# Delta rule: the mixer's taps on ScalarE and VectorE, and the projections as three fp32r products

## The chip, the cores and the metric

The kernel runs on one core of a Trainium2 chip. The metric is the device time of one execution in microseconds; lower is better. Engines are called by the profile's short names: PE (TensorE), PEld (its weight loads), ACT (ScalarE), DVE (VectorE), POOL (GpSimd), SP (SyncE, which here only issues transfers).

## What is computed

The reference is one transformer block on x of shape (8, 512, 256): attention with a bias from a small MLP, then a gated delta rule, then two mixtures of experts. The change lies in the delta rule; of it, this matters here (h is the attention's output, one batch of 512 rows by 256):

```python
def short_conv(x, w):                # 4 taps per channel
    ...
    return y * jax.nn.sigmoid(y)
def fractal_mixer(x, conv_w):
    out = 2.0 * x
    for i in range(4):
        dil = 2 ** i
        x_shift = jnp.pad(x, ((0, 0), (dil, 0), (0, 0)))[:, :l, :]
        out = out + x_shift * conv_w[i, :, 0] + x * conv_w[i, :, 1]
    return out
q = short_conv(x @ Wq, conv_q)       # k and v in the same way
...                                  # rotary, l2norm, chunks of 32 rows:
S_new = g * S + k.T @ (u - w @ S)    # one state per head, 16 chunks in a row
...
frac = rmsnorm(fractal_mixer(x, frac_conv_w), mixer_norm_w)
```

## The kernel before, in words

Three phases follow one another: attention (0 to 1094 us of the profiled span), the delta rule (1099 to 1750) and the mixtures (1755 to the end). `attention_phase` writes its output turned, as `hT`, to DRAM; `delta_phase` reads one batch of it at a time into `h` (two buffers), with the 256 channels as two blocks (`KD`) of 128 partitions and the 512 rows along the free dimension.

`delta_phase` is a pipeline over the eight batches. Each engine works through a hand-written list of named pieces (`PE_ROUND`, `ACT_ROUND`, `DVE_ROUND`, `POOL_ROUND`, L1825 to L1876), once per round, in exactly that order. An entry (name, i, lag) works in round r on batch r - lag: lag NX = -1 is the next batch (first four projections, gates), IN = 0 the batch that comes in, F = 1 the one after it (inverse, u and w), R = 2 the recurrence, K = 3 the output. Twelve rounds run, from -1 to 10; rounds 3 to 6 hold pieces of every lag. The engines meet only through semaphores, so a piece that waits holds up all that stands behind it on its engine. PE's results go through a ring of five PSUM banks (`RING`) in PE's order: a bank is filled again once its reader is through.

The pieces that matter:

- "step" i on PE (L2126) and "S" i on DVE (L2406) are the recurrence over 16 chunks. Step i waits for S i-1, S i for step i. All other pieces stand between them.
- "proj" (L1978): a projection is 2 matmuls in fp32 (one for each block of channels), which the profile shows as 4 MATMULs of 512 columns. ACT copies it to `proj` and makes the first tap of the convolution (L2189, L2193); "conv" on DVE adds three more (L2292); "silu" on ACT.
- "mixer" (L2001): for each of 4 row tiles and 2 channel blocks, 5 matmuls of h, shifted by 1, 2, 4, 8 and 0 rows, against diagonal matrices `diag` of the taps, so that the sum comes out turned, rows on partitions. The profile shows 20 MATMULs for a tile. ACT's "frac" reads it (sum of squares, copy to `xg`), then "fve" on DVE, "frs" on POOL, and "xg" on DVE. All are IN pieces.
- After the projections: "z" (turn q and k), "rota"/"rotb" on DVE (L2304, L2316) and "rot" on POOL (rotary; rotb needs POOL's part, L2319), "rsq" (ACT), "rss" (DVE), "rrn" (POOL), "qk" (DVE), "qkT" (PE turns, ACT copies), "gram" (PE), "low" (DVE, L2355). SP then sends `low` through DRAM into `A0`, POOL inverts it ("inv", L2496, the last piece of POOL's list), and SP brings the result back as `TT1` for "T1", "Z" and "TZ" of the next round. POOL's next round begins with "kb", "gxm", "ors", "nb" and then "rot".
- "core" (PE) and "x1" (DVE) are the output of batch r - 3; `vk` (values and scaled keys) has two buffers.

Of the kernel before, what the change touches and what calls it, by code (L numbers as in the profile page):

```python
# [97 lines left out]
def delta_inputs(nc, ctx, a, sem):  # L98
# [5 lines left out]
    t = {"wqkv": sb("wqkv", [P, KD, 3 * D]), "wsm": sb("wsm", [P, KD, NG]), "smb": sb("smb", [P, NG]),  # L104
# [16 lines left out]
    t["in"], t["h0_in"], t["loads"] = sem("delta_in"), sem("delta_h0_in"), loads  # L121
    return t
# [15 lines left out]
def attention_phase(nc, a, ident, delta, mixture, bias_rows, hT_dram, inv_dram):  # L138
# [6 lines left out]
    with ExitStack() as ctx:  # L145
# [197 lines left out]
        with nc.Block() as block:  # L343
# [227 lines left out]
            def _(dve):  # L571
# [28 lines left out]
                for name, t in steps:  # L600
# [158 lines left out]
                    elif name == "hn":  # L759
                        dve.wait_ge(s["out_rstd"], t + 1)  # L760
                        if t > 0:
                            dve.wait_ge(full[1], filling["hT", t - 1, 1])
                        dve.tensor_scalar(hn[:], FB[0][:, 0:D], mv2[:, 0:1], rstd2[:], ALU.subtract,
                                          ALU.mult).then_inc(s["hn_ready"], 1)

            @block.scalar
            def _(act):
# [26 lines left out]
                for name, t in steps:  # L794
# [96 lines left out]
                    elif name == "hT":  # L891
# [6 lines left out]
                        last.then_inc(s["hT_ready"], 1)  # L898

# [772 lines left out]
def delta_phase(nc, a, ident, delta, mixture, hT_dram, xg_dram, low_dram, inv_dram, x1_dram):  # L1672
# [5 lines left out]
    with ExitStack() as ctx:  # L1678
        sb, bank, sem, sems = space(nc, ctx, "d")
        wqkv, wsm, smb, conv, frac, cos, sin, rot, mixw, strict, causal, chunk_of, side, eye16, corner, wo, onw, x = (  # L1680
            delta[n] for n in ("wqkv", "wsm", "smb", "conv", "frac", "cos", "sin", "rot", "mixw", "strict", "causal",
                               "chunk_of", "side", "eye16", "corner", "wo", "onw", "x"))
        own = sb("own", [P, KD])
        diag = sb("diag", [P, KD, 5, P])
# [3 lines left out]
        half = sb("half", [P, TT * H2])  # L1688
        h = [delta["h0"], sb("h1", [P, KD, PAD + L])]
        xg = sb("xg", [P, TT, D])  # L1690
# [5 lines left out]
        fsq = sb("fsq", [P, TT, D])  # L1696
# [27 lines left out]
        vk = sb("vk", [P, 2, TT, H2, 2, DH])  # L1724
# [27 lines left out]
        x_in = sem("x_in")  # L1752
        proj_psum = sem("proj_psum")
# [7 lines left out]
        nb_ready = sem("nb_ready")  # L1761
        mixer_psum = sem("mixer_psum")
# [60 lines left out]
        NS = NCH - 1  # L1823

        PE_ROUND = [  # L1825
            ("step", 0, R), ("fast", 0, R), ("M", 1, R), ("qp", 0, R), ("proj", 4, IN), ("au", 0, R),
            ("step", 1, R), ("fast", 1, R), ("M", 2, R), ("mixer", 0, IN), ("M", 3, R),
# [3 lines left out]
            ("step", 5, R), ("fast", 5, R), ("hold", 0, K), ("hold", 1, K), ("hold", 2, K), ("hold", 3, K), ("onT", 0, K), ("onT", 1, K), ("z", 3, IN), ("mixer", 1, IN),  # L1831
            ("step", 6, R), ("fast", 6, R), ("TZ", 0, F), ("core", 0, K), ("au", 3, R),
            ("step", 7, R), ("fast", 7, R), ("qkT", 0, IN), ("uw", 0, F), ("attn", 0, F),
            ("step", 8, R), ("fast", 8, R), ("mixer", 2, IN), ("qkT", 1, IN), ("uw", 1, F),
            ("step", 9, R), ("fast", 9, R), ("core", 1, K), ("qkT", 2, IN), ("uw", 2, F),
            ("step", 10, R), ("fast", 10, R), ("mixer", 3, IN), ("uw", 3, F), ("qkT", 3, IN),
# [7 lines left out]
            ("M", 2, R), ("osq", 0, K), ("silu", 2, IN), ("M", 3, R), ("frac", 0, IN),  # L1844
# [3 lines left out]
            ("onT", 0, K), ("onT", 1, K), ("z", 3, IN), ("rsq", 1, IN), ("frac", 1, IN),  # L1848
# [20 lines left out]
            ("S", 12, R), ("attn", 2, F), ("low", 1, IN), ("attn", 3, F), ("xg", 0, IN),  # L1869
            ("S", 13, R), ("vb", 0, IN), ("conv", 0, NX), ("xg", 1, IN),  # L1870
            ("S", 14, R), ("vb", 1, IN), ("conv", 1, NX), ("xg", 2, IN), ("gates", 0, NX), ("xg", 3, IN)]
        POOL_ROUND = [
            ("kb", 0, F), ("gxm", 0, F), ("ors", 0, K), ("nb", 0, IN), ("rot", 0, IN), ("rot", 1, IN), ("rrn", 0, IN),
            ("rot", 2, IN), ("rrn", 1, IN), ("rot", 3, IN), ("rrn", 2, IN), ("rrn", 3, IN), ("frs", 0, IN),
# [5 lines left out]
        def drained(name, i, b):  # L1880

            return {"fast": None, "hold": None, "proj": (proj_ready, 6 * b + i + 1), "gates": (gates_read, b + 1),
                    "mixer": (frac_copied, TT * b + i + 1), "z": (zm_ready, TT * b + i + 1),
# [21 lines left out]
        with nc.Block() as block:  # L1905
            @block.sync
            def _(sp):
                for r_ in range(B + 3):
                    bi, bf, bk = r_, r_ - 1, r_ - 3
                    if bi < B - 1:  # L1910
                        if bi > 0:
                            sp.wait_ge(mixer_psum, TT * bi)
                        sp.dma_start(h[(bi + 1) % 2][:, :, PAD:], hT_dram[bi + 2]).then_inc(h_in[(bi + 1) % 2], 16)
# [36 lines left out]
                    if bi < B:  # L1950
# [316 lines left out]
            def _(dve):  # L2267
# [19 lines left out]
                for name, i, b in pieces(DVE_ROUND):  # L2287
# [308 lines left out]
```

## Time and profile before

| what | us |
|---|---|
| median of 3 runs (lowest to highest) | 2610.37 (2606.3 to 2613.95) |
| the profiled execution: its time | 2605.69 |
| its span, first to last instruction | 2603.9 |
| PE busy | 2413.8 (93%) |
| DVE busy | 1696.0 (65%) |
| POOL busy | 1334.0 (51%) |
| ACT busy | 1216.3 (47%) |

Shares are of the whole span. A busy PE is one with matmuls under way; their ends are modelled. A row of a timeline reads: start, duration, engine, line, operation, output<-inputs, shape, count, and in brackets the idle time of the engine before it and what ended that. In a row that merges several instructions the duration is from the first one's start to the last one's end. A table by windows gives for each stretch the busy time of every engine with its count of instructions, then the granted clock of PE (1.00 is 2.4 GHz, 0.50 is 1.2 GHz).

### The profile page before, as it was taken

The page shows a single profiled execution, that of the slowest core. Times are in us where ns is not written, and L with a number is a line of the kernel's source. Part 1 is how long each engine was busy: PE and PEld are TensorE (multiplying, and loading weights), DVE is VectorE, ACT ScalarE, POOL GpSimd, SP SyncE. Part 2 cuts the span into 40 slices and gives each one's busy share as a digit, 9 for nine tenths or more (in the row PEclk, how much of TensorE's full clock was granted, in tenths as well). Part 3 has the DMA queues.
Part 4 walks back from the last instruction along what each step waited for, and adds up shares of the span by engine and source line. Part 5 has one row for each costly group of instructions (what it writes and reads, how often), then busy time and mean ns, then how long its engine had stood idle before and what let it go on. Part 6 is the DMA issues. An engine that isn't in the chain of part 4 may idle for free. (4 is left out here: it accounts for less than half of the span.)

```text
span 2603.9 us, 56605 instructions
## 1 busy us (share of the span) xinstructions
PE 2413.8 (93%) x20854; PEld 2007.2 (77%) x20854; DVE 1696.0 (65%) x4060; ACT 1216.3 (47%) x3095; POOL 1334.0 (51%) x1465
## 2 busy tenths in 40 slices
PE   4899999999999999878999999988899999999998
PEld 3788888888888888756777877756677778778776
DVE  4576777767677767576767767326756746747664
ACT  2656666666666666455444445114333333332332
POOL 3676776767676767256555555214522323322322
PEclk8999999999999999989999999988999999999999
DMA  4000100000000000012112111206112112212211
GB/s 141 7 10 9 45 17 11 9 10 10 10 10 9 9 5 5 15 31 45 42 47 49 36 53 43 55 31 187 33 52 68 62 42 74 66 42 62 64 39 58
DMA packets 156688, 105.05 MB, mean 40 GB/s; under 512 B 85168, under 2 KB 134832, under 8 KB 156416
## 3 DMA queue, kind: packets, MB, share of 16 engines
q1 hardware_dynamic: 131072, 62.83, 8.9%
q10 hardware_dynamic: 25344, 38.60, 4.8%
q8 instruction: 170, 2.79, 0.4%
q14 instruction: 102, 0.84, 0.1%
HBM read 80.51 MB, written 20.88 MB: 39 GB/s over the span
## 5 line engine op out<-in xcount | busy, mean ns | idle before, releaser
L920 POOL TENSOR_TENSOR a_bm<-a_bias,a_mask_add 128x512 f32<-128x512 f32 (+3 forms) x512 | 437.8, 871 | 191.0 <-DVE a_nm L674 186.0
L1529 POOL TENSOR_TENSOR m_hid_part<-m_hid,m_hid_part 128x512 fp32r<-128x512 f32 x176 | 239.5, 1361 | 564.1 <-ACT m_hid_part L1438 561.0
L830 ACT ACTIVATE a_S<-a_S,a_nm 128x512 f32<-128x512 f32 (+3 forms) x512 | 289.2, 565 | 346.4 <-DVE a_nm L674 343.6
L674 DVE CUSTOM_DVE_ANT_0 a_S<-a_S,a_bm,a_nsn 128x512 f32<-128x512 f32 (+3 forms) x512 | 275.4, 545 | 141.2 <-PE a_S L438 136.9
L461 PE MATMUL a_O<-a_v,a_PT 128*128 128x64 f32 x2560 | 342.4, 265 | 0.0
L461 PEld LDWEIGHTS a_O<-a_v,a_PT 128*128 128x128 f32 x2560 | 328.4, 193 | 0.0
L1450 ACT ACTIVATE m_hid<-m_G 128x512 f32<-128x512 f32 x176 | 105.4, 599 | 408.4 <-PE m_G L1384 371.3
L438 PE MATMUL a_S<-a_kT,a_qT 128*128 128x384 f32 (+3 forms) x1024 | 284.3, 359 | 3.5 <-DVE a_nm L674 3.0
L1401 PE MATMUL m_Y<-m_hid_part,m_down_high 128*128 128x512 f32 x704 | 257.3, 406 | 11.9 <-POOL m_hid_part L1529 11.1
L1611 DVE TENSOR_TENSOR m_hid<-m_hid,m_U 128x512 f32<-128x512 f32 x176 | 121.0, 687 | 223.6 <-PE m_U L1384 189.7
L1384 PE MATMUL m_G<-m_in,m_gate_high 128*128 128x512 f32 x704 | 251.5, 398 | 1.6 <-POOL m_up_low L1523 1.6
L1384 PE MATMUL m_U<-m_in,m_up_high 128*128 128x512 f32 x704 | 250.8, 397 | 1.7 <-DVE m_hid L1611 1.7
L448 PE MATMUL a_T<-s_ident,a_S 128*128 128x128 f32 x1280 | 227.0, 275 | 12.2 <-ACT a_PT L839 11.3
L448 PEld LDWEIGHTS a_T<-s_ident,a_S 128*128 128x128 f32 x1280 | 160.3, 140 | 42.2 <-ACT a_S L830 15.7
L438 PEld LDWEIGHTS a_S<-a_kT,a_qT 128*128 128x128 f32 x1024 | 164.1, 192 | 18.7 <-DVE a_nm L674 6.5
L1401 PEld LDWEIGHTS m_Y<-m_hid_part,m_down_high 128*128 128x128 f32 x704 | 133.4, 189 | 47.7 <-issue 15.8
L1384 PEld LDWEIGHTS m_U<-m_in,m_up_high 128*128 128x128 f32 x704 | 132.8, 189 | 34.9 <-DVE m_hid L1611 2.8
L1384 PEld LDWEIGHTS m_G<-m_in,m_gate_high 128*128 128x128 f32 x704 | 133.0, 189 | 34.5 <-POOL m_up_low L1523 2.1
L839 ACT COPY a_PT<-a_T 128x128 f32<-128x128 f32 (+3 forms) x384 | 156.2, 407 | 0.0
L1384 PE MATMUL m_G<-m_in,m_gate_low 128*128 128x512 f32 x352 | 140.2, 398 | 0.0
L1401 PE MATMUL m_Y<-m_hid_part,m_down_low 128*128 128x512 f32 x352 | 139.8, 397 | 0.0
L525 PE MATMUL a_F<-a_wqkv,a_xnT 128*128 128x512 f32 (+1 forms) x576 | 133.8, 369 | 5.9 <-POOL a_wqkv L944 3.7
(314 smaller groups left out, 5240.2 us busy)
## 6 DMA issues: line engine op xcount, KB each, us to landing
m_spread<-s_w ACTq DMA_DIRECT2D x64, 256.0 KB, 3.3
m_spread<-s_w ACTq DMA_DIRECT2D x128, 128.0 KB, 2.9
a_x<-in_x SPq DMA_DIRECT2D x32, 128.0 KB, 2.1
s_hT<-a_hT SPq DMA_DIRECT2D x32, 128.0 KB, 2.1
d_x<-in_x SPq DMA_DIRECT2D x8, 512.0 KB, 4.8
d_h<-s_hT SPq DMA_DIRECT2D x8, 512.0 KB, 5.4
s_xg<-d_xg SPq DMA_DIRECT2D x8, 512.0 KB, 3.1
d_x<-s_xg SPq DMA_DIRECT2D x8, 512.0 KB, 4.5
```

The lines of the kernel that those rows point to most:

```text
L438: last = pe.matmul(o_s[:, 0:w], qT[:, tile % 2, h], kT[tile // TT % 2][i][:, 0:w], start=i == 0, stop=i == 1)
L448: last = pe.transpose(TB[n % 2][:, j * P:(j + 1) * P], S[:, n % S_SLOTS, j * P:(j + 1) * P], ident[:])
L461: last = pe.matmul(OB[h // 8][:, (h % 8) * DH:(h % 8 + 1) * DH], PT[:, n % PT_SLOTS, j * P:(j + 1) * P], v[tile // TT % 2][:, j], start=j ...
L525: last = pe.matmul(f[:, 0:cols.stop - cols.start], xnT[i][:, k], wqkv[j][:, k, cols], start=n == 0, stop=n == len(terms) - 1)
L674: dve.tensor_tensor_reduce(S[:, n % S_SLOTS, 0:w], SB[n % 2][:, 0:w], bm[:, n % BM_SLOTS, 0:w], -1.0, nsn[:, tile % 2, h:h + 1], ALU.add, ...
L830: act.activation(S[:, n % S_SLOTS, 0:w], S[:, n % S_SLOTS, 0:w], ACT.Exp, scale=-1.0, bias=nm[:, tile % 2, h:h + 1], accum_out=den[:, tile ...
L839: act.copy(PT[:, n % PT_SLOTS, 0:w], TB[n % 2][:, 0:w]).then_inc(s["probsT_act"], 1)
L920: pool.tensor_tensor(bm[:, n % BM_SLOTS, 0:w], bias[:, h, L - w:L], mask_add[b % 2][:, 0:w], ALU.add).then_inc(s["bm_ready"], 1)
L1384: last = pe.matmul(dst[q % 2][:, :], wts[m][j][:, k, item], x[i][:, k], start=(i, j, k) == TERMS[0], stop=(i, j, k) == TERMS[-1])
L1401: last = pe.matmul(YB[k][:, :], down[m][j][:, item, k * P:(k + 1) * P], hid_part[i][:, q % H_SLOTS], start=item == 0 and i + j == 0, stop= ...
L1529: pool.tensor_tensor(hid_part[1][:, q % H_SLOTS], hid[:, q % G_SLOTS], hid_part[0][:, q % H_SLOTS].bitcast(F32), ALU.subtract).then_inc(hi ...
L1611: dve.tensor_tensor(h, h, UB[q % 2][:, :], ALU.mult).then_inc(mult_up, 1)
```

## The change

The mixer's sum is made by ACT (the unshifted tap, scaled, into a new buffer `mx`) and DVE (four shifted taps added in place); PE only turns `mx`. PE's turning, "frac", "fve", "frs" and "xg" move to lag F, one round later. The projections take both operands as fp32r, split into a high part (the cast) and a low part (the rest): high by high, weights' low by high, high by the input's low, so 6 matmuls of 512 columns. The input is split once a batch by two pieces "hs": ACT casts the high part, DVE subtracts it. The weights are split once, during attention. `vk` keeps one buffer, which "vb" and "kb" fill once "uw" of the batch before has been read.

```diff
@@ attention_phase, DVE and ACT
+                        if t == 4 * TT:      # behind "hn"
+                            dve.wait_ge(delta["high_ready"], 1)
+                            dve.tensor_tensor(delta["w_low"][:], delta["wqkv"][:], delta["w_high"][:].bitcast(F32),
+                                              ALU.subtract).then_inc(delta["low_ready"], 1)
...
+                        if t == 3 * TT:      # behind "hT"
+                            act.wait_ge(delta["in"], 16 * len(delta["loads"]))
+                            act.copy(delta["w_high"][:], delta["wqkv"][:]).then_inc(delta["high_ready"], 1)
@@ PE_ROUND: mixer 0 to 3 keep their places, IN becomes F
-            ("step", 10, R), ("fast", 10, R), ("mixer", 3, IN), ("uw", 3, F), ("qkT", 3, IN),
+            ("step", 10, R), ("fast", 10, R), ("mixer", 3, F), ("uw", 3, F), ("qkT", 3, IN),
@@ ACT_ROUND: frac 0 to 3 become F, and
-            ("frac", 2, IN), ("qkT", 1, IN), ("uw", 1, F),
-            ("qkT", 2, IN), ("uw", 2, F), ("silu", 5, IN),
-            ("frac", 3, IN), ("uw", 3, F), ("qkT", 3, IN),
+            ("frac", 2, F), ("qkT", 1, IN), ("uw", 1, F), ("tap", 0, IN),
+            ("hs", 0, NX), ("qkT", 2, IN), ("uw", 2, F), ("silu", 5, IN),
+            ("tap", 1, IN), ("frac", 3, F), ("uw", 3, F), ("qkT", 3, IN),
@@ DVE_ROUND: fve and xg become F, and
-            ("S", 9, R), ("qk", 3, IN), ("conv", 5, IN),
-            ("S", 10, R), ("x1", 1, K),
-            ("S", 11, R), ("fve", 0, IN), ("attn", 1, F), ("low", 0, IN),
+            ("S", 9, R), ("qk", 3, IN), ("hs", 0, NX), ("conv", 5, IN),
+            ("S", 10, R), ("x1", 1, K), ("mix", 0, IN),
+            ("S", 11, R), ("fve", 0, F), ("attn", 1, F), ("low", 0, IN), ("mix", 1, IN),
             ("S", 12, R), ("attn", 2, F), ("low", 1, IN), ("attn", 3, F), ("xg", 0, F),
@@ SP: the load of h waits for mix, proj and gates instead of the mixer; xg goes out one round later
@@ PE
+                        if i == 0:
+                            pe.wait_ge(h_high, b + 1)
+                            pe.wait_ge(h_low, b + 1)
                         o = fill(name, i, b)
-                        for k in range(KD):
-                            last = pe.matmul(o[:, :], wqkv[:, k, i * P:(i + 1) * P], h[b % 2][:, k, PAD:],
-                                             start=k == 0, stop=k == KD - 1)
+                        for n, (j, s, k) in enumerate(TERMS):
+                            last = pe.matmul(o[:, :], wqkv[j][:, k, i * P:(i + 1) * P], h_part[s][:, k],
+                                             start=n == 0, stop=n == len(TERMS) - 1)
...
                     elif name == "mixer":
+                        pe.wait_ge(mix_ready, KD * (b + 1))
                         o = fill(name, i, b)
                         for k in range(KD):
-                            ...
+                            last = pe.transpose(o[:, k * P:(k + 1) * P], mx[:, k, i * P:(i + 1) * P], ident[:])
                         last.then_inc(mixer_psum, 1)
@@ ACT
+                def input_high(b):
+                    if b == 0:
+                        act.wait_ge(delta["h0_in"], 16)
+                    else:
+                        act.wait_ge(h_in[b % 2], 16 * ((b + 1) // 2))
+                        act.wait_ge(proj_psum, 6 * b)
+                    act.copy(h_part[0][:], h[b % 2][:, :, PAD:]).then_inc(h_high, 1)
+                input_high(0)
...
+                    elif name == "tap":
+                        if b == 0:
+                            ...
+                        else:
+                            act.wait_ge(h_in[b % 2], 16 * ((b + 1) // 2))
+                            act.wait_ge(mixer_psum, TT * b)
+                        act.activation(mx[:, i], h[b % 2][:, i, PAD:], ACT.Copy, scale=own[:, i:i + 1]).then_inc(mix_tap, 1)
@@ DVE
+                def input_low(b):
+                    dve.wait_ge(h_high, b + 1)
+                    dve.tensor_tensor(h_part[1][:], h[b % 2][:, :, PAD:], h_part[0][:].bitcast(F32),
+                                      ALU.subtract).then_inc(h_low, 1)
...
+                    elif name == "mix":
+                        dve.wait_ge(mix_tap, KD * b + i + 1)
+                        for j in range(4):
+                            at = PAD - 2 ** j
+                            ins = dve.scalar_tensor_tensor(out=mx[:, i], in0=h[b % 2][:, i, at:at + L],
+                                                           scalar=frac[:, i, j, 0:1], in1=mx[:, i],
+                                                           op0=ALU.mult, op1=ALU.add)
+                            ...
```

Also gone: the ten VectorE instructions that build `diag` once (L2278). "frac" now copies first and squares in place in PSUM.

## Rows read from the trace of the kernel before

**Rows 1.** Busy time by windows: steady round 4, and round 6.

```profile
1356.70:1427.70 71.00, 70.82 (x1282) 56.20 (x1280) 50.59 (x109) 35.00 (x76) 41.18 (x61) 1.00 0.20 51
1498.80:1573.20 74.40, 73.97 (x1281) 57.86 (x1278) 50.49 (x109) 35.07 (x76) 40.47 (x58) 0.95 0.19 48
```

**Rows 2.** Timeline of SP: low leaves in rounds 0, 1, 2, 4; last, inverse done.

```profile
1149.30 0.39 SPq L1941 DMA_DIRECT2D s_low<-d_low  x1
1206.38 0.37 SPq L1941 DMA_DIRECT2D s_low<-d_low  x1
1272.00 0.37 SPq L1941 DMA_DIRECT2D s_low<-d_low  x1
...
1414.04 0.36 SPq L1941 DMA_DIRECT2D s_low<-d_low  x1
...
1435.03 1.31 SPq L1924 DMA_DIRECT2D s_inv<-d_AT  x2
```

**Rows 3.** Timeline of POOL in round 4: kb, ors, last part of rot 0.

```profile
1364.76 2.78 POOL L2484 TENSOR_TENSOR d_vk<-d_qk,d_gates 128x256 f32<-128x256 f32 x4
...
1369.39 3.34 POOL L2518 TENSOR_TENSOR d_ors<-d_oss,d_half 128x16 f32<-128x16 f32 x1 [1.46 <-DVE d_oss L2423]
...
1376.84 0.73 POOL L2466 TENSOR_TENSOR d_rb<-d_rb 128x256 f32<-128x256 f32 x1
```

**Rows 4.** Timeline of DVE: qk 3 of round 0, rotb 0 of round 1, pieces of round 4.

```profile
1142.22 0.69 DVE L2340 TENSOR_TENSOR d_qk<-d_r,d_rrn 128x512 f32<-128x512 f32 x1 [1.53 <-POOL d_rrn L2472]
...
1178.56 0.42 DVE L2324 TENSOR_TENSOR d_r<-d_zm,d_ra 128x256 f32<-128x256 f32 x1 [8.66 <-POOL d_rb L2466]
...
1377.82 0.41 DVE L2324 TENSOR_TENSOR d_r<-d_zm,d_ra 128x256 f32<-128x256 f32 x1
...
1396.46 0.69 DVE L2340 TENSOR_TENSOR d_qk<-d_r,d_rrn 128x512 f32<-128x512 f32 x1
...
1412.61 0.47 DVE L2416 SCALAR_TENSOR_TENSOR d_S<-d_S,d_gm,d_state 128x64 f32<-128x64 f32 x2 [2.11 <-PE d_state L2145]
1413.00 0.68 DVE L2394 TENSOR_TENSOR d_attn<-d_R,d_causal 128x512 f32<-128x512 f32 x1
1413.60 0.41 DVE L2362 TENSOR_TENSOR d_low<-d_R,d_nb 128x256 f32<-128x256 f32 x1
```

**Rows 5.** Windows over round 4 for the mixer's line alone, then the projections' line (PE, PEld, clock).

```profile
1356.70:1427.70 71.00, 9.89 (x80) 9.23 (x80) 1.00 0.20 51
1356.70:1427.70 71.00, 11.68 (x24) 4.08 (x24) 1.00 0.20 51
```

**Rows 6.** Timeline of PE: six fp32r matmuls in the mixtures (start to start of the next group).

```profile
2004.80 0.40 PE L1384 MATMUL m_G<-m_in,m_gate_high 128*128 128x512 f32 x1
...
2006.21 0.40 PE L1384 MATMUL m_U<-m_in,m_up_high 128*128 128x512 f32 x1
```

**Rows 7.** Timeline of PE in round 4: steps 9 and 10, mixer 3.

```profile
1397.51 0.45 PE L2137 MATMUL d_state<-d_uw,d_qk 32*64 32x64 f32 x8
...
1401.98 0.45 PE L2137 MATMUL d_state<-d_uw,d_qk 32*64 32x64 f32 x8
...
1403.08 2.50 PE L2007 MATMUL d_R<-d_diag,d_h 128*128 128x128 f32 x20
```

**Rows 8.** Groups of instructions of the delta phase (busy, mean ns | idle before).

```profile
L2292 DVE SCALAR_TENSOR_TENSOR d_y<-d_proj,d_conv,d_y 128x512 f32<-128x512 f32 x144 | 111.5, 775 | 7.2 <-ACT d_y L2193 3.8
L2193 ACT ACTIVATE d_y<-d_proj,d_conv 128x512 f32<-128x512 f32 x48 | 34.7, 723 | 1.6
L2426 DVE TENSOR_TENSOR d_oc<-d_oc,d_ors 128x1024 f32<-128x1024 f32 x8 | 10.8, 1346 | 10.3 <-POOL d_ors L2518 10.3
L2261 ACT ACTIVATE d_osq<-d_oc 128x1024 f32<-128x1024 f32 x8 | 8.4, 1048 | 0.0
```

**Rows 9.** Busy time by windows of 2 us in round 8, at and behind an idle stretch of PE.

```profile
1655.00:1657.00 2.00, 0.00 (x0) 0.00 (x0) 0.00 (x0) 0.00 (x0) 2.00 (x1) 1.00 0.29 48
1659.00:1661.00 2.00, 2.00 (x136) 1.94 (x125) 1.42 (x4) 0.00 (x0) 0.00 (x0) 0.50 0.33 129
```

More of the change, by code:

```diff
@@ L1688, in delta_phase @@
         half = sb("half", [P, TT * H2])
+        wqkv = [delta["w_high"], delta["w_low"]]
         h = [delta["h0"], sb("h1", [P, KD, PAD + L])]
+        h_part = [sb(f"h_part{j}", [P, KD, L], mybir.dt.float32r) for j in range(2)]
         xg = sb("xg", [P, TT, D])
@@ L1761, in delta_phase @@
         nb_ready = sem("nb_ready")
+        own_ready = sem("own_ready")
+        mix_tap = sem("mix_tap")
+        mix_ready = sem("mix_ready")
         mixer_psum = sem("mixer_psum")
@@ L1823, in delta_phase @@
         NS = NCH - 1
+        TERMS = [(j, s, k) for j, s in ((0, 0), (1, 0), (0, 1)) for k in range(KD)]
         PE_ROUND = [
             ("step", 0, R), ("fast", 0, R), ("M", 1, R), ("qp", 0, R), ("proj", 4, IN), ("au", 0, R),
-            ("step", 1, R), ("fast", 1, R), ("M", 2, R), ("mixer", 0, IN), ("M", 3, R),
+            ("step", 1, R), ("fast", 1, R), ("M", 2, R), ("mixer", 0, F), ("M", 3, R),
             ("step", 2, R), ("fast", 2, R), ("M", 0, R), ("au", 1, R), ("z", 0, IN),
@@ L2001, in _ @@
                     elif name == "mixer":
+                        pe.wait_ge(mix_ready, KD * (b + 1))
                         o = fill(name, i, b)
                         for k in range(KD):
-                            at = PAD + i * P
-                            for j in range(5):
-                                back = 0 if j == 4 else 2 ** j
-                                last = pe.matmul(o[:, k * P:(k + 1) * P],
-                                                 h[b % 2][:, k, at - back:at - back + P], diag[:, k, j],
-                                                 start=j == 0, stop=j == 4)
+                            last = pe.transpose(o[:, k * P:(k + 1) * P], mx[:, k, i * P:(i + 1) * P], ident[:])
                         last.then_inc(mixer_psum, 1)
@@ L2273, in _ @@
                 link(dve.tensor_reduce(own[:], frac[:, :, :, 1], AX.X, ALU.add))
-                link(dve.tensor_scalar(own[:], own[:], 2.0, None, ALU.add))
-                for k in range(KD):
-                    for i in range(5):
-                        w = own[:, k:k + 1] if i == 4 else frac[:, k, i, 0:1]
-                        dve.tensor_scalar(diag[:, k, i], ident[:], w, None, ALU.mult)
+                dve.tensor_scalar(own[:], own[:], 2.0, None, ALU.add).then_inc(own_ready, 1)
                 dve.wait_ge(rot_ready, 1)
@@ L2287, in _ @@
                 for name, i, b in pieces(DVE_ROUND):
-                    if name == "conv":
+                    if name == "hs":
+                        if b > 0:
+                            input_low(b)
+                    elif name == "conv":
                         w = conv[:, i // 2, i % 2]
```

83 lines of the change are left out of this document (49 added, 34 removed).

## The prediction

> **What bounds the kernel now.** I read the table by windows first, then the timelines of the engines through one steady round. In round 4 PE is busy 70.82 of 71.00 us at the full clock, DVE 50.59, POOL 41.18, ACT 35.00 [rows 1]. So PE bounds the steady rounds, and what is taken from PE looks like gain. The second look is at what comes close behind. There is a chain that closes on itself once a round. DVE's "rotb" 0 needs POOL's "rot" 0; from there it goes over the norms, "qkT" and "gram" to "low"; SP sends `low` out, POOL inverts it as the last piece of its list, and only behind that come "kb", "gxm", "ors", "nb" and the next "rot" 0. Its lengths: from rotb 0 at 1377.82 [rows 4] to the issue of low at 1414.04 [rows 2] 36.2 us; from there to the inverse at 1435.03 [rows 2] 21.0; from the start of kb at 1364.76 to the end of rot 0 at 1376.84 + 0.73 [rows 3] 12.8, of which 1.46 is a wait of ors; 0.25 more to rotb. Together 70.3, in a round of 71.0. POOL is little over half busy, and still its chain has only some 2 us of slack: the wait of ors and the rest to 71.0. In round 1, where PE has no recurrence yet, this chain is the bound outright: DVE waits 8.66 us for POOL's rot [rows 4].
>
> **The change part by part.** *PE.* A tile of the mixer's matmuls takes 9.89 / 4 = 2.47 us [rows 5]; in its place come two turns, which I price as two of the 20 matmuls that take 2.50 [rows 7], 0.25 (between nothing and the tile they replace). That is 2.22 less, four times: 8.9 a round. A projection takes 11.68 / 6 = 1.95 [rows 5]; six fp32r matmuls take 2006.21 - 2004.80 = 1.41 [rows 6], so 0.54 less, six times: 3.2. PE's work falls by 12.1 to 58.9 us a round.
>
> *DVE and ACT.* DVE gets eight taps of 0.775 [rows 8], 6.2 a round, and hs, a tensor_tensor over 1024 elements: 1.35 by L2426 [rows 8]. ACT gets two taps of 0.72 and a cast of 1024 elements, 1.05 by L2261 [rows 8]: 2.5. DVE comes to some 58 us; neither is full by its sum.
>
> *The wait that is added.* It is in the order. "tap" 0 waits for mixer_psum of the whole batch before, since `mx` has one buffer: for mixer 3, which PE reaches behind step 10 of the same round. ACT works in order, so behind that wait stand hs, qkT 2, uw 2, silu 5, tap 1, frac 3, uw 3 and qkT 3. DVE's hs waits for ACT's hs, and behind it stand conv 5, S 10, x1 1 and mix 0. PE's step 11 needs S 10, and its qkT 3 a bank that x1 1 empties. I follow this through with rotb 0 left at 1377.82. DVE is through qk 2 at 1396.46 + 0.69 as before [rows 4]. Step 9 loses the mixer tile before it: 1397.51 - 2.2 = 1395.3; step 10 follows 4.47 later, at 1399.8; mixer 3 another 1.10 later [rows 7], done at 1401.2. Then tap 0 to 1401.9, hs on ACT to 1403.0, hs on DVE to 1404.3, conv 5 (3 x 0.775) to 1406.6, S 10 (0.47) to 1407.1, x1 1 (0.68, as attn) to 1407.8. PE has nothing to do from uw 3 (its end, some 1402.3) until then: an idle stretch of about 5 us. On DVE follow mix 0 (4 x 0.775), S 11, fve and attn 1 (0.47 + 0.16 + 0.68), low 0 (0.41), mix 1 (3.1), S 12, attn 2 and low 1 (0.47 + 0.68 + 0.41): 1417.3. These instructions overlap by some 0.05 to 0.08 each (1412.61 + 0.47 against 1413.00 [rows 4]), so I take 1416.5. low leaves 2.5 us later behind rotb 0 than before, 38.7 instead of 36.2.
>
> *The chain, summed again.* 38.7 + 21.0 + 11.4 (ors no longer waits: the inverse comes later in PE's round) + 0.25 = 71.4 us. PE's 12.1 us are all given back. The ends: if every DVE and ACT price is a quarter lower, 2.5 us of it go, and the round is 69; if hs and the taps stretch as much as some conv 5 do beside POOL (half a microsecond each), it is 73.
>
> *The clock.* PE now idles about 5 us before step 11 and some 4 before step 6, which waits for the S 5 behind rotb 0. In round 8 PE has an idle stretch, 0.00 busy from 1655 to 1657, and behind it the granted clock is 0.50, the lower of its levels (1.2 GHz), with PE fully busy [rows 9]. Rounds 3 to 5 pay nothing of this today (1.00), and round 6, at 0.95, is 74.4 us instead of 71.0 [rows 1], as is round 7. Price of two drops a round: nothing if they fall into waits, 3.4 (round 6) if all of it lies on the chain; the steps behind both stretches lie on it in part, so I take half, 1.8. A steady round: 73.2.
>
> The Trainium skill has a rule here that speaks against the change: TensorE: Matmul & The Clock Gate, in "HAM oscillation — how this bites in real kernels", says that a wait between bursts of matmuls sends the clock down and that the burst behind each such wait starts slow. The trace agrees for one stretch [rows 9]. By the rule every steady round pays that price in full, and a round would be 74.8, some 8 us more over five rounds; the steady rounds of now alone, which pay nothing [rows 1], would leave it at 71.4.
>
> *The first rounds.* Start: one cast and one subtraction (1.05 + 1.35) stand ahead of the first projection, which is then shorter: +1 at conv 0. Round 0: low 1 follows qk 3 behind hs, conv 5, mix 0, low 0, mix 1 (1.35 + 2.3 + 3.1 + 0.4 + 3.1 + 0.4 = 10.6), where now it comes 6.4 behind it (1149.30 against 1142.22 + 0.69 [rows 2, 4]): +4.2. Round 1 (57.1 from 1149.30 to 1206.38 [rows 2]), on the POOL chain already: the same 4.2, and tap 0 and the cast on ACT (0.72 + 1.05) between mixer 3 and DVE's hs: +6.0. Round 2 (65.6, to 1272.00 [rows 2]): the chain of 71.4 without ors (3.34 [rows 3]) and the two x1 (1.3) is 66.8 to 67.4: +1.8 at most, and +1 for the clock.
>
> *The rest.* Rounds 3 to 7 are 3 x 71.0 + 2 x 74.4 = 362 now and 5 x 73.2 = 366 then: +4. Rounds 8 to 10 start from the last low; four pairs of turns stand in round 8: +1. The split of the weights, 1536 elements on ACT and DVE once (1.5 and 2 by rows 8), lies in attention beside PE's work; between 0 and 3.5, I take 0.5. The load of h and xg on SP keep their places at the round's ends; `vk` with one buffer is refilled after uw 3 was read, long before: nothing, unless the round were much shorter. The ten instructions for `diag` go, under conv's cover: nothing.
>
> **Sum.** 1 + 4.2 + 6.0 + 2.8 + 4 + 1 + 0.5 = +19.5 us. The profiled execution took 2605.69, its span 2603.9; the median of the runs is 4.7 above it. On the profiled one that is 2625.2; between that and the median's 2630 I forecast **2627**.
>
> **The rivals.** (a) *Faster: the POOL chain does not bind.* POOL's spans are rough, and 71.4 stands on a sum of many. If it were 5 us shorter, the steady round is PE's 58.9 plus the 5 us in which it waits for S 10, plus 2.5 for mix 1 ahead of S 12: 66.4. Five rounds 332 instead of 362, the first rounds +10: about 2590. For it: POOL busy 41 of 71. Against: round 1's wait. It decides from a chain under 68. (b) *Faster: all of PE's saving arrives.* Six rounds of 12.1: about 2538. It needs tap 0 not to wait, which the order excludes as I read it. (c) *No change:* the clock stays up and the waits of the first rounds are half hidden: +13.1 / 2 - 5 x 1.0 + 1.5, about 2614. (d) *Slower still: the clock.* If PE fell to 1.2 GHz for some 14 us of each steady round, with every step on the chain, a round takes about 77: 2646. It decides from the point at which the second stretch's slow matmuls reach step 12. The one fall whose price shows cost 3.4 us [rows 1], which speaks against it. (e) *fp32r runs no faster behind fresh weights:* 6 x 0.1 us a projection more. It falls into PE's idle time: it would show in the rows and not in the time.
>
> **How the numbers follow.** The forecast (2615 to 2638) 0.54, (a) 0.13, (b) 0.05, (c) 0.18, (d) 0.10. The measurement tells 0.3% (8 us, so 2602 and 2618) from no change. Faster: (a) and (b), 0.18. Within: most of (c) and the foot of the forecast, 0.18. Slower: 0.64. The range takes in (a)'s edge, (c), the forecast and most of (d): 2592 to 2646. The forecast's own, without the faster cases, is 2615 to 2646.
>
> **What would show it.** Right: steady rounds (low to low) of 71 to 75 us with PE busy some 60; ACT idle before tap 0, ended by PE's turns of mixer 3; DVE idle before hs by ACT; PE idle before step 11; rotb 0 waiting for POOL in every round; a granted clock below 1.00 in rounds 3 to 5. low to low of about 63 in round 1. Wrong: steady rounds of 60 to 67, or a rotb 0 that does not wait for POOL.

## The result, and the profile after

The changed kernel takes 2670.08 us (median of 4 runs, 2658.16 to 2672.74); the kernel before took 2611.56 in the same comparison. The ratio is 1.0225, 95% interval 1.0199 to 1.0251: slower, as forecast, but by 59 us and not by 17. The profiled execution took 2672.74, its span is 2670.9, 67.0 more than before. Cut at the issues of `low` on SP, these 67 us lie here (us; "rest" is from the last `low` to the end of the span):

| stretch | before | after | difference | forecast |
|---|---|---|---|---|
| to the first low | 1149.3 | 1153.9 | +4.6 | +5.7 |
| round 1 | 57.1 | 61.4 | +4.3 | +6.0 |
| round 2 | 65.6 | 77.4 | +11.8 | +2.8 |
| rounds 3 to 7 | 362.1 | 392.3 | +30.3 | +4 |
| rest | 969.8 | 985.8 | +16.0 | +1 |

The windows of the changed kernel (length, busy time of PE, PEld, DVE, ACT, POOL, then the granted clock): one whole round, from low to low, and three stretches inside it.

```profile
1535.12:1613.62 78.50, 71.55 (x1217) 58.49 (x1216) 58.26 (x118) 36.60 (x78) 41.61 (x59) 0.83 0.19 46
1558.00:1568.00 10.00, 10.00 (x87) 8.30 (x86) 7.93 (x13) 5.02 (x14) 9.92 (x14) 0.51 0.48 95
1597.00:1599.00 2.00, 0.00 (x0) 0.00 (x0) 1.61 (x2) 1.33 (x3) 0.00 (x0) 1.00 0.00 0
1599.00:1616.00 17.00, 14.01 (x204) 11.29 (x205) 11.58 (x23) 3.25 (x8) 2.49 (x3) 0.50 0.18 45
```

Before, a round was 71.0 us with PE busy all through it at the full clock [rows 1]. Now it is 78.5 (rounds 3, 5 and 6; round 4 takes 85.2, round 7 71.5), and PE is busy 71.55 of it although some 10 us of its work at the full clock are gone (below, under prices): the clock is 0.83. It is at the lower level twice. Once from 1599 for 17 us, behind an idle stretch; that one was looked for. And once from 1558 for 10 us, with PE busy 10.00 of 10.00 and, in the 20 us ahead of it, no wait of PE over 0.21; that one was not. The timelines show the idle stretch (start, length, in brackets the idle time before and what ended it): PE first, then ACT, then DVE.

```profile
1595.17 0.44 PE L2027 MATMUL d_R<-s_ident,d_mx 128*128 128x128 f32 x2
1595.54 1.07 PE L2081 MATMUL d_R<-d_vk,d_inv 32*32 32x128 f32 x32
1601.99 1.09 PE L2049 MATMUL d_R<-s_ident,d_qk 128*128 128x128 f32 x4 [5.37 <-DVE d_x L2486]
1603.00 0.69 PE L2155 MATMUL d_state<-d_uw,d_qk 32*64 32x64 f32 x8
```

```profile
1595.70 0.72 ACT L2232 ACTIVATE d_mx<-d_h,d_own 128x512 f32<-128x512 f32 x1 [4.58 <-PE d_R L2027]
1596.33 1.03 ACT L2202 CAST d_h_part<-d_h 128x1024 fp32r<-128x1024 f32 x1
```

```profile
1597.39 1.23 DVE L2310 TENSOR_TENSOR d_h_part<-d_h,d_h_part 128x1024 fp32r<-128x1024 f32 x1 [3.91 <-ACT d_h_part L2202]
1598.54 2.32 DVE L2336 SCALAR_TENSOR_TENSOR d_y<-d_proj,d_conv,d_y 128x512 f32<-128x512 f32 x3
1600.77 0.47 DVE L2470 SCALAR_TENSOR_TENSOR d_S<-d_S,d_gm,d_state 128x64 f32<-128x64 f32 x2
1601.15 0.68 DVE L2486 TENSOR_TENSOR d_x<-d_R,d_x 128x512 f32<-128x512 f32 x1
1601.76 3.10 DVE L2345 SCALAR_TENSOR_TENSOR d_mx<-d_h,d_frac,d_mx 128x512 f32<-128x512 f32 x4
```

Read it as a relay: the turns of mixer 3 on PE, tap 0 and the cast on ACT, the difference, conv 5, S 10 and x1 on DVE, and then PE again, 5.37 us idle. The first group of step 11 takes 0.69, where that of step 9 took 0.45 before [rows 7]: the same work takes longer, it doesn't only start later.

The other reading concerns rotb 0 and POOL's rot 0. First POOL, then DVE:

```profile
1567.36 1.59 POOL L2520 TENSOR_TENSOR d_rb<-d_rb 128x256 f32<-128x256 f32 x1
```

```profile
1570.22 0.47 DVE L2470 SCALAR_TENSOR_TENSOR d_S<-d_S,d_gm,d_state 128x64 f32<-128x64 f32 x2 [1.85 <-PE d_state L2163]
1571.59 0.69 DVE L2456 SCALAR_TENSOR_TENSOR d_qpT<-d_R,d_qkT 128x512 f32<-128x512 f32 x1 [0.89 <-PE d_R L2119]
1572.19 0.41 DVE L2378 TENSOR_TENSOR d_r<-d_zm,d_ra 128x256 f32<-128x256 f32 x1
```

POOL's part is there at 1568.95; rotb 0 starts at 1572.19, behind S 4 and qp, which waited for PE. For 3.2 us the ring over POOL had slack, and PE at the lower clock set the pace.

### The profile page after: what moved, and what is told of

The parts are those of the page before. It is cut to its first block and busy times, and to the rows that moved or that the text cites. A ratio compares the mean times of both kernels' runs of the same rounds, so it can differ in the third digit from the quotient of the medians.

```text
span 2670.9 us, 55799 instructions
## 1 busy us (share of the span) xinstructions
PE 2424.3 (91%) x20374; PEld 2032.0 (76%) x20374; DVE 1753.7 (66%) x4123; ACT 1231.4 (46%) x3120; POOL 1337.9 (50%) x1465
## 5 line engine op out<-in xcount | busy, mean ns | idle before, releaser
L1414 PE MATMUL m_Y<-m_hid_part,m_down_high 128*128 128x512 f32 x704 | 258.2, 408 | 12.6 <-POOL m_hid_part L1542 11.8
L454 PE MATMUL a_T<-s_ident,a_S 128*128 128x128 f32 x1280 | 227.0, 275 | 12.1 <-ACT a_PT L849 11.3
```

Of the source, the lines that this page charges most:

```text
L454: last = pe.transpose(TB[n % 2][:, j * P:(j + 1) * P], S[:, n % S_SLOTS, j * P:(j + 1) * P], ident[:])
L1414: last = pe.matmul(YB[k][:, :], down[m][j][:, item, k * P:(k + 1) * P], hid_part[i][:, q % H_SLOTS], start=item == 0 and i + j == 0, stop= ...
```

## The experiments

The theory: most of the loss is PE's clock, which falls behind the new wait and also where dense matmuls were taken from between small ones. The rival: it is the wait itself, by the order on ScalarE. A third: the ring over POOL, as forecast. The ratio of each kernel is to the kernel before, timed beside it; runs of one kernel spread by up to 29 us, so only the ratios with their intervals decide, and stages are read from one profiled execution each. Several edits put in fillers: `unread(o, n)` runs n matmuls of 512 columns in bf16 whose sums nobody reads, some 0.22 us each at the full clock. Both kernels have such fillers already, in the pieces "fast" (two behind each step of round 8, one in round 9) and "hold" (round 10), and none in rounds 3 to 7.

**The order mended.**

```diff
-("uw", 1, F), ("tap", 0, IN), ("hs", 0, NX), ("qkT", 2, IN), ("uw", 2, F), ("silu", 5, IN),
+("uw", 1, F), ("qkT", 2, IN), ("uw", 2, F), ("silu", 5, IN), ("tap", 0, IN),
-("qkT", 0, IN), ("uw", 0, F), ("rsq", 3, IN),
+("hs", 0, NX), ("qkT", 0, IN), ("uw", 0, F), ("rsq", 3, IN),
```

> The changed kernel with two entries of ScalarE's order moved: the cast of the next input stands two places earlier, ahead of the first qk turn, and tap 0 stands behind the last silu, next to tap 1. So conv 5 and S 10 wait for no mixer tile any more. Order theory: TensorE's idle 5 us before step 11 are gone, the clock stays up behind step 11 too, rounds fall by 5 to 8 us to 71 to 73, 2610 to 2630 us. Clock theory: the idle time goes, but the fall in steps 2 to 4, which has no idle time ahead of it, stays, and more falls come where dense matmuls are missing: granted clock 0.80 to 0.92, rounds of 73 to 77 us, 2635 to 2660 us.

Measured: 2615.10 us, ratio 1.0017 (0.9996 to 1.0038). Two entries of a list give 55 us of the 59 back; the order theory's number came out. But its picture of the clock did not:

```profile
1500.19:1570.12 69.93, 68.42 (x1215) 55.80 (x1216) 58.09 (x118) 36.29 (x79) 41.40 (x59) 0.88 0.21 51
```

The idle stretch before step 11 is down from 21.5 us in four rounds to 3.2, the round is at 69.9, and the clock is still 0.88. In this execution rounds 1 to 7 took 478.9 us against 484.8 before and 531.1 in the changed kernel; the first low came at 1160.6, and the rest took 979.4. So the rounds gained 5.9 us, and the start and the tail cost 20.9 (this profiled execution is one of the slower of its kernel, the one before one of the faster).

**The cast alone moved** (tap 0 stays ahead of qkT 2).

> The changed kernel with one of the two entries moved: the cast of the next input stands ahead of the first qk turn; tap 0 stays ahead of the third qk turn, where it waits for the last mixer tile. If the path from that wait through cast, difference and conv 5 to S 10 is what costs: idle time before step 11 under 1 us, 2612 to 2625 us, as with both moved. If what costs is the work queued behind tap 0 on ScalarE itself (the third qk turn, uw, silu 5): 2640 to 2670 us, with the idle time still there.

Measured: 2631.43 us, 1.0061 (1.0032 to 1.0089), spread from 2617 to 2640; between both cases. Most of the 55 us come with the cast, some 39, the rest with tap 0's own place. In the profiled execution, one of the shortest (2617.97), PE waited 5.0 us before step 11 in four rounds, at most 1.4, where the changed kernel waited 21.5: as in the first case. Where the rest lies it doesn't show.

**PE kept busy in the wait.** The changed kernel, its order and its wait as they are:

```diff
 elif name == "uw":
     o = fill(name, i, b)
+    unread(o, 20 if i == 3 else 0)
```

> The changed kernel in its own order, with one thing added: 20 unread matmuls of 512 columns, 4.3 us at the full clock, in front of the last tile's uw matmuls, which is where TensorE then waits 5.4 us for S 10; it is kept busy in the wait, and the wait is as long as before. It tells the price of the wait itself from that of the clock that falls behind it (0.50 for 16 us of each round). If the clock behind the idle time is what costs: step 11 no later, the clock from it on at 1.00, rounds of 70 to 73 us in place of 78.5, 2615 to 2635 us. If the wait itself costs the time, whatever the clock does behind it: rounds of 77 us and more, 2655 to 2685 us.

Measured: 2645.32 us, 1.0136 (1.0103 to 1.0169): 25 of the 59 us gone, between the two cases. First the waits of PE from 1290 to 1640 (engine, tile, line, what was waited for: us in total, times, longest), the changed kernel and then this one; then the 17 us in this one that begin 2.5 us before PE's next work, as those from 1599 do by 3 us in the changed kernel.

```profile
PE d_R L2049 <- DVE d_x L2486: 21.5, 4, 5.4
```

```profile
PE d_R L2049 <- DVE d_x L2487: 4.2, 4, 1.1
```

```profile
1498.00:1515.00 17.00, 15.94 (x314) 12.68 (x311) 15.92 (x33) 5.65 (x12) 2.77 (x3) 1.00 0.25 53
```

PE's next work came no earlier for the filling, 6.8 us behind the turns of mixer 3 in both kernels, as it hangs on DVE; but the clock behind it was 1.00 in place of 0.50. Rounds 1 to 7 took 499.6 us where the changed kernel's took 531.1 and the mended order's 478.9: of the 52.2 us between these two, 31.5 went with the clock behind the wait. (The profiled execution is the shortest of its four, the changed kernel's the longest of its four; by the medians it is 25 of 55.) So the wait is the cause, and about half of its price is paid behind it, at 1.2 GHz. With the clock up, most rounds wait for the ring over POOL. POOL's rot 0 and DVE's rotb 0 in round 6 of this kernel:

```profile
1542.71 0.73 POOL L2521 TENSOR_TENSOR d_rb<-d_rb 128x256 f32<-128x256 f32 x1
```

```profile
1543.53 0.42 DVE L2379 TENSOR_TENSOR d_r<-d_zm,d_ra 128x256 f32<-128x256 f32 x1 [0.16 <-POOL d_rb L2521]
```

rotb 0 starts 0.09 us behind POOL's part (0.10 in round 3, 0.2 in round 5, 1.0 in round 4, 2.5 in round 7), where it was 3.2 in the changed kernel.

**Matmuls put back where they were taken out**, in the changed kernel's order.

```diff
 elif name == "mixer":
+    unread(o, 10)
 if name == "proj":
+    unread(o, 2)
```

> The changed kernel, with matmuls whose sums nobody reads put where matmuls were taken out: 10 of 512 columns in front of each tile's two mixer turns, 2 in front of each projection, 52 in a round, some 11 us of TensorE at its full clock. Clock theory (TensorE falls to 1.2 GHz since the change took dense matmuls from between the steps, and all that it does then takes twice as long): granted clock above 0.95 in rounds 3 to 7 in place of 0.76 to 0.83, rounds of 71 to 74 us, 2615 to 2635 us in all. Order theory (the wait of tap 0 for the last mixer tile, and the cast and conv 5 behind it, cost the time, and the clock only follows from the idle 5 us): the idle 5 us before step 11 stay, and the clock falls behind them as now, so 2660 to 2690 us.

Measured: 2704.01 us, 1.0365 (1.0333 to 1.0397). A miss for the clock theory as it stood.

```profile
1469.09:1554.51 85.42, 79.53 (x1270) 61.33 (x1269) 57.19 (x118) 36.97 (x78) 42.43 (x59) 0.88 0.17 42
```

The clock only rose from 0.83 to 0.88; the idle 21.5 us in four rounds stayed to the tenth, and ten more matmuls stand ahead of mixer 3's turns, on the very path by which tap 0 waits. A filler is work: in front of what others wait for it can cost more than it gives, here 34 us against the changed kernel.

**The two halves of the change.** The mixer's half: projections in fp32 from the unsplit weights, no cast, no difference. The projections' half: the mixer's 80 matmuls back, its copies in the round of the input.

```diff
 # mixer's half
-for n, (j, s, k) in enumerate(TERMS):
-    last = pe.matmul(o[:, :], wqkv[j][:, k, i * P:(i + 1) * P], h_part[s][:, k], ...)
+for k in range(KD):
+    last = pe.matmul(o[:, :], delta["wqkv"][:, k, i * P:(i + 1) * P], h[b % 2][:, k, PAD:], ...)
 # projections' half
-    last = pe.transpose(o[:, k * P:(k + 1) * P], mx[:, k, i * P:(i + 1) * P], ident[:])
+    for j in range(5):
+        last = pe.matmul(o[:, k * P:(k + 1) * P], h[b % 2][:, k, at - back:at - back + P], diag[:, k, j], ...)
```

> The mixer's half of the change alone: the projections are two fp32 products each from the unsplit weights and input, as before the change, and the splits (weights, input) are gone; the mixer is on ScalarE and VectorE. If the mixer's half carries the loss (8.4 us of matmuls less in a round, tap 0's wait): 2640 to 2665 us, granted clock under 0.90. If the projections' half carries it (3 us of TensorE less, cast and difference of the input between conv and step): 2605 to 2625 us. If the loss is shared by size of the PE work removed: about 2650 us.

> The other half alone: the mixer is the 80 fp32 matmuls in a round that it was, with its tables of diagonals, and its sums are copied in the round of the input; the projections are six fp32r products from the split weights and input, the cast stands ahead of the third qk turn and the difference ahead of conv 5. If the mixer's half carries the loss: within 10 us of the kernel before, 2600 to 2622 us, clock of rounds 3 to 5 near 1.00. If the projections' half carries it: 2640 to 2665 us. Here no tap waits for a mixer tile, so the order theory wants less than 1.5 us of idle time before step 11.

Measured: the mixer's half 2632.95 us, 1.0089 (1.0056 to 1.0123); the projections' half 2610.53, 0.9995 (0.9977 to 1.0013). The loss of the halves is 19 and none, and of both together 59: the cast and the difference are harmless unless they stand behind tap 0's wait, and only together do the halves make the relay above. From 1290 to 1640 PE waits for another engine at most 0.8 us at a time in the first and 0.4 in the second. The mixer's half is also the clean case of a clock that falls without a wait. Its windows from step 1 on:

```profile
1312.00:1316.00 4.00, 4.00 (x108) 3.42 (x106) 3.43 (x6) 3.96 (x7) 0.24 (x2) 1.00 0.65 138
1316.00:1326.00 10.00, 10.00 (x87) 7.36 (x83) 7.22 (x13) 4.98 (x13) 7.15 (x8) 0.51 0.34 80
```

and PE at the beginning of it:

```profile
1313.14 1.15 PE L2125 MATMUL d_R<-d_qk,d_uw 32*64 32x64 f32 x32
1314.22 0.44 PE L2022 MATMUL d_R<-s_ident,d_mx 128*128 128x128 f32 x2
1314.59 0.97 PE L2125 MATMUL d_R<-d_qk,d_uw 32*64 32x64 f32 x26
```

PE is busy without a gap. Between two rows of 32x64 matmuls stands a pair of turns of 0.44 us where before stood a tile of 2.50 [rows 7], and the clock falls 2 us later. No wait stands ahead of it. That the missing tile has to do with it is shown by the next kernel.

**Fillers in the mended order**, first 5 in front of every mixer tile's turns:

> The kernel with the two moved entries, and 5 unread matmuls in front of the turns of every mixer tile, 20 in a round, 4.3 us. Clock theory: granted clock of rounds 3 to 7 from 0.90 to above 0.97; since a round of 69 to 70 us is then set by VectorE, GpSimd and the inverse's transfers, it stays 69 to 70, and what is won lies in rounds 1, 2 and 8: 2600 to 2612 us. Rival (TensorE's work lies on the path of a round, so that each matmul put back costs its own time, as the first kernel with fillers suggests): rounds of 72 to 74 us, 2625 to 2645 us.

Measured: 2615.61 us, 1.0007 (0.9988 to 1.0025), against 2615.10 without. The clock of the later rounds rose to 0.93 to 0.98 and the rounds stayed at 69 to 71. The same stretch of round 5, some 18 us behind low, without the fillers (the mended order) and with them:

```profile
1448.00:1461.00 13.00, 13.00 (x134) 10.73 (x134) 9.20 (x15) 6.61 (x16) 12.29 (x19) 0.50 0.38 71
```

```profile
1447.00:1460.00 13.00, 12.82 (x206) 10.43 (x201) 9.51 (x17) 9.83 (x23) 12.29 (x19) 1.00 0.36 71
```

This fall takes 10 to 14 us in each of rounds 3 to 7 without the fillers. With them it takes 10 in round 3 (in two parts), 7 in rounds 4 and 7, and is not there in rounds 5 and 6. So matmuls in the place of the missing tile shorten it or keep it away. But it didn't set the time: rounds 1 to 7 took 479.6 us against 478.9. In rounds 4 to 6 rotb 0 starts 0.1 to 0.2 us behind POOL's part; in round 6 DVE waits for it. The chain of the first case sets the round, though the time lies between both cases:

```profile
1533.94 0.42 DVE L2379 TENSOR_TENSOR d_r<-d_zm,d_ra 128x256 f32<-128x256 f32 x1 [2.18 <-POOL d_rb L2521]
```

**Fillers at the ends of the work.** Eight in front of each mixer tile of the last two inputs; then of the first two as well, with 4 in front of their projections.

> The kernel with the two moved entries of ScalarE's order, and 8 unread matmuls of 512 columns in front of the two turns of each mixer tile of the last two inputs alone (rounds 7 and 8), where dense matmuls stood before the change. Clock theory for the tail: TensorE's clock, which fell to 1.2 GHz 3 us before the last store of low with no wait ahead of it and stayed there for 36 us, stays at 2.4 GHz; from the last store of low to the end 979 us become 968 to 973, in all 2603 to 2609 us. Rival (the tail is longer since the mixer's turns and its sums now stand in round 8, whatever the clock): 978 us or more, 2613 to 2622 us.

> The kernel with the two moved entries, with 8 unread matmuls in front of the turns of each mixer tile of the first two and the last two inputs, and 4 in front of each projection of the first two inputs; rounds 3 to 6 without any. Clock theory: the first store of low 3 to 5 us earlier than without (the granted clock of round 0 and 1 was 0.70 against 0.91 before the change), the tail 6 to 11 us shorter: 2598 to 2607 us, which would beat both kernels. Rival: what is put back costs as much as the clock gives, 2612 to 2625 us.

Measured: 2627.58 us, 1.0053 (1.0028 to 1.0078), and 2627.23, 1.0060 (1.0029 to 1.0090): by the ratios some 9 and 11 us slower than without (1.0017), with intervals that still overlap, and both outside of what was expected. In the first one's profile the clock fell at the end of round 7 all the same, for 20 us where it was 38 without, there behind a wait of PE of 1.37 us; round 8, with 32 fillers in it, took 64.8 us against 63.7 from the copy of one batch's output to the next. So the shorter fall bought nothing.

**The split of the weights moved** to the last two tiles of the attention, for the projections' half (with the cast early) and for the mended order.

```diff
-if t == 3 * TT:        # ScalarE's cast of the weights
+if t == B * TT - 2:
-if t == 4 * TT:        # VectorE's difference
+if t == B * TT - 1:
```

> The projections' half alone (mixer on TensorE as before the change), with the cast of the next input two places earlier on ScalarE, and the split of the weights moved from the fourth and fifth batch of the attention to its last two tiles, where ScalarE and VectorE wait. If the split in mid-attention delayed the attention (its last store of the normed rows came 3.6 us later in that half's profile): 3 to 5 us less than the 2610.5 us of that half, 2604 to 2608 us, just faster than the kernel before. If those 3.6 us are the spread from run to run: 2608 to 2614 us, no difference.

> Both halves of the change with the two moved entries of ScalarE's order (2615.1 us before), and the split of the weights moved to the last two tiles of the attention. If the split in mid-attention costs: 2609 to 2613 us. If not: 2613 to 2618 us. Round 8, 8 us longer than in the kernel before, stays as it is in both cases.

Measured: 2606.76 us, 0.9987 (0.9965 to 1.0009), and 2613.22, 1.0010 (0.9992 to 1.0027). The medians are 4 and 2 us lower than without the move, the first inside what was expected if the split costs, the second between the two cases; but the intervals of the ratios overlap with those without it, and the first kernel has the cast moved as well: not settled.

**Fourteen matmuls at one place.** The last kernel above, with fillers in round 7 alone:

```diff
 elif name == "attn":
+    unread(o, 4 if i >= 2 and b == B - 2 else 0)
 elif name == "v":
+    unread(o, 3 if b == B - 1 else 0)
```

> The kernel of the last run but with unread matmuls at one place of the whole work: 4 in front of each of the last two attn pieces and 3 in front of each v piece at the end of round 7, 14 in all, 3 us of TensorE, where the clock fell to 1.2 GHz for 36 us without any wait ahead of it. The matmuls in the last two rounds are otherwise those of the last run. If the clock is why round 8 takes 8 us longer than before the change: the fall does not come, or comes later and shorter, round 8 (from the copy of one batch's output to the next) falls from 63.8 to 56 to 60 us, 2605 to 2611 us. If the work that the change moved into round 8 is why: 64 us and more as before, 2613 to 2619 us.

Measured: 2604.23 us against 2612.52, ratio 0.9967 (0.9952 to 0.9983). It is the one version whose interval lies below 1: faster than both kernels, by 8 us or a third of a per cent. The windows without the fillers, then with them:

```profile
1634.00:1644.00 10.00, 9.64 (x88) 7.57 (x84) 7.30 (x18) 0.18 (x1) 1.27 (x1) 0.55 0.31 41
1644.00:1676.00 32.00, 32.00 (x439) 24.63 (x438) 8.92 (x21) 5.05 (x10) 14.24 (x36) 0.50 0.29 80
```

```profile
1634.00:1644.00 10.00, 10.00 (x144) 7.50 (x143) 7.60 (x21) 1.86 (x4) 2.83 (x6) 1.00 0.35 53
1644.00:1661.00 17.00, 13.52 (x242) 10.45 (x240) 5.42 (x13) 3.29 (x7) 12.60 (x31) 1.00 0.48 119
1661.00:1669.00 8.00, 7.67 (x183) 6.22 (x185) 1.78 (x4) 1.83 (x5) 0.00 (x0) 0.57 0.13 52
```

Without them the clock falls at 1635 with PE busy 9.64 of 10.00 and stays down for 40 us; with 3 us of matmuls it stays up, until an idle stretch sends it down for 7 us, as one did before [rows 9]. Round 8, from the copy of one batch's output to the next, falls from 63.8 to 57.1 us (55.5 before the change). The changed kernel has such a fall too, 2 us behind a wait of PE of 0.80 us:

```profile
1682.00:1721.00 39.00, 39.00 (x412) 29.80 (x400) 14.52 (x37) 5.24 (x11) 15.49 (x37) 0.50 0.32 76
```

**The same in every round.**

> The 14 unread matmuls of the last run in front of attn 2, attn 3 and the v pieces, now in every round in place of round 7 alone, 3 us of TensorE a round; all else as there (2604.2 us). If the falls of the clock that are left in rounds 1 to 6 (granted clock 0.70 to 0.92) set these rounds' length: rounds 1 and 2 two to five us shorter (60.3 and 70.3 us there, 57.1 and 65.6 before the change), the later ones at 68 to 70, 2594 to 2601 us. If the rounds are set by the chain over VectorE, GpSimd and the inverse's transfers, with TensorE in their shadow: no difference, 2602 to 2608 us. If each matmul put back lies on the path, as in the first kernel with fillers: 3 us a round more, 2618 to 2628 us.

Measured: 2630.53 us, 1.0068 (1.0043 to 1.0093). The third case, and a little beyond it: rounds 1 to 7 take 501.1 us against 481.7. The loss isn't even: of these 19.4 us 10.2 fall on round 3, and the others take 0.8 to 3.0 more each, round 7, where both kernels have the fillers, 1.2. The clock is lower in round 3 (0.91 without them) and higher in round 6 (0.85 without):

```profile
1283.72:1363.13 79.41, 76.50 (x1231) 60.38 (x1230) 59.05 (x118) 36.56 (x78) 40.40 (x59) 0.82 0.19 45
1508.12:1580.67 72.55, 70.25 (x1232) 56.49 (x1231) 57.95 (x118) 36.91 (x79) 40.42 (x59) 0.91 0.20 49
```

In rounds 3 to 6 rotb 0 starts 2.2 to 5.7 us behind POOL's part, without these fillers 0.1 to 1.8. So the ring over POOL does not set the pace here, in keeping with the third case; yet the 20 fillers in front of the mixer tiles cost nothing in the same order. The place makes the difference, and why this one costs was not followed.

## Why the prediction was right and wrong

The side was right, and so was the wait that the change adds. What bounds a round was not, nor the size, and the time lies outside the range.

*Prices: right but for PE's.* The groups of the changed kernel from 1099 to 1821 (count, busy and mean ns, idle before):

```profile
L2345 DVE SCALAR_TENSOR_TENSOR d_mx<-d_h,d_frac,d_mx 128x512 f32<-128x512 f32 x64 | 48.0, 750 | 1.8
...
L2232 ACT ACTIVATE d_mx<-d_h,d_own 128x512 f32<-128x512 f32 x16 | 11.4, 715 | 31.4 <-PE d_R L2027 31.4
L2310 DVE TENSOR_TENSOR d_h_part<-d_h,d_h_part 128x1024 fp32r<-128x1024 f32 x8 | 9.8, 1224 | 32.6 <-ACT d_h_part L2202 32.6
L2202 ACT CAST d_h_part<-d_h 128x1024 fp32r<-128x1024 f32 x8 | 8.2, 1031 | 5.3 <-PEq L53 5.3
```

Taps at 0.75 and 0.72, the difference at 1.22 (1.35 by [rows 8]), the cast at 1.03 (1.05). A pair of turns takes 0.37 from its start to the next (0.25 was said). A projection at the full clock, from its start to the next row, before and in the changed kernel:

```profile
1346.97 1.88 PE L1983 MATMUL d_R<-d_h,d_wqkv 128*128 128x512 f32 x4
1348.78 0.45 PE L2137 MATMUL d_state<-d_uw,d_qk 32*64 32x64 f32 x8
```

```profile
1544.45 0.71 PE L2005 MATMUL d_R<-d_h_part,d_wqkv_high 128*128 128x512 f32 x2
...
1546.03 0.41 PE L2172 MATMUL d_O<-d_S,d_qpT 64*32 64x64 f32 x8
```

That is 1.58 where 1.81 to 1.92 stood; the forecast set 1.41, from start to start in the mixtures, against 1.95, a busy time. So PE's work falls by some 10 us a round and not by 12.1; an estimate, 4 x 2.1 for the mixer's tiles and 6 x 0.3.

*The wait: right.* Tap 0 behind mixer 3, and behind it cast, difference, conv 5, S 10, x1: "about 5 us" of idle PE are 5.37, with the same pieces in the same order. That it is the cause is shown by the mended order. Of the other signs the fall of the clock in rounds 3 to 5 came (0.83, 0.76, 0.83); rounds of 71 to 75 us, PE busy some 60 and rotb 0 waiting for POOL did not.

*The clock: the step that failed.* "Price of two drops a round: nothing if they fall into waits, 3.4 (round 6) if all of it lies on the chain; ... so I take half, 1.8. A steady round: 73.2." The drops were not of that size. The row for 3.4 was that of a round with one short fall (0.95); here the clock is down for some 27 us of a round, and keeping it up behind the wait alone gave 31.5 us over seven rounds, 4.5 each, in the profiled executions, and 25 in all by the medians. Rounds 3 to 7 took 392.3 us, with the wait filled 366.6, and 366 was forecast. That the last two agree is in part luck, as the filled kernel has 4.3 us of fillers a round and still some falls (0.91 in round 5). The upper bound was taken from the one fall that the trace showed. The second fall, without any wait, was not in the sum at all.

*The ring over POOL: not the bound of the changed kernel.* SP's row on the inverse of its round 6:

```profile
1557.46 1.31 SPq L1946 DMA_DIRECT2D s_inv<-d_AT  x2
```

The ring's terms came out as 41.4 from rotb 0 to low (38.7 was said), 22.3 to the inverse (21.0), 11.5 to the end of rot 0 (11.4 and 0.25), and 3.2 more in which rotb 0 waited not for POOL but for S 4: 78.5 and not 71.4. "rotb 0 waiting for POOL in every round" was named as a sign, and it isn't there; its absence was named as a sign of being wrong. It is there once the clock is kept up: in round 6 of the kernel with the filled wait rotb 0 starts 0.09 us behind POOL, 38.9 us lie from it to low, and the round takes 73.2. So the ring was added up nearly right, and it was the clock that lifted the round above it. Where the 1.3 us between low and the inverse come from was not followed.

*The rest: the other term that failed.* "Rounds 8 to 10 start from the last low; four pairs of turns stand in round 8: +1" measured +16.0. Round 8 alone, from copy to copy, took 62.7 us against 55.5. What was left out is the long fall of the clock that begins at the end of round 7. It comes with the mixer's half: that half alone has it (43 us, round 8 63.6), the projections' half has a fall of 3 us and 56.5. In the mended kernel 14 unread matmuls at that place took 6.7 us off round 8. Which of the moved pieces the clock missed is not shown: 8 matmuls in the tiles' old places left a fall of 20 us. The other 9 of the 16 us were not followed.

*Start and rounds 1 and 2.* +5.7 and +6.0 against +4.6 and +4.3 are near, and not better known than that: the first low of the mended kernels' profiles comes anywhere from 1151 to 1165. Round 2, +2.8 against +11.8, failed by the same clock (0.74 from 1215 to 1293, 1.00 before). The split of the weights at 0.5 is not settled, as said.

*Rivals.* (d) had the mechanism and, at 77 us a round for 14 us at the lower clock, came nearest (78.5 and 27); it was given 0.10 because "The one fall whose price shows cost 3.4 us". (a) to (c) fell. Two slips of the sums change nothing: half of 3.4 is 1.7, and the 13.1 for the first rounds in (c) is 13.0 by the terms given.

The Trainium skill's rule that was weighed (TensorE: Matmul & The Clock Gate, "HAM oscillation — how this bites in real kernels") says that a burst of matmuls behind a wait starts at the lower clock. The runs agree: behind the wait of 5.37 us the clock was 0.50, and 1.00 with the wait filled. The 74.8 us a round that the prediction worked out by it are nearer than 73.2 and still 4 short of 78.5.

## What to carry to other kernels

Taking dense matmuls from an engine that is full removes more than their time: look at what is left to run in their places, and price a fall of the clock by all that would run at the lower clock behind it, not by the one fall that the old trace happens to show. Before a wait on one engine's ordered list is accepted, ask whether the entry behind it needs that wait; here moving two entries was worth 55 us. Matmuls put in to hold the clock gave 25 us in an existing wait and some 9 at the place where a long fall begins, changed nothing in front of the mixer's tiles of the mended order, and lost 9 to 34 us elsewhere, so each place is a measurement of its own.

## What was not expected of the hardware

In the kernel with the mixer's half alone the granted clock fell to 0.50 with PE busy 10.00 of 10.00 us and no wait ahead, where a tile of 2.50 us between rows of 32x64 matmuls had become two turns of 0.44. With 5 unread matmuls in front of such turns, in the mended order, the fall was shorter or gone (0.50 and 1.00 in the two windows of round 5). So a profile that shows PE busy without a gap does not show that the clock is up. And the clock can stay down long: 39 us with PE busy 39.00 of 39.00 in the changed kernel from the end of round 7, while 14 matmuls (3 us) at the same place in the mended kernel avoided 40 us at the lower clock.
